# A mixture-of-experts block on one core: one-hot list products laid out tile by tile, with four experts' lists made ahead

## What is computed

```python
logits = flat_x @ gate_w.T
scores = softmax(logits, axis=-1).T               # (16, 8192)
topk_weight, topk_idx = top_k(scores, C)          # each expert picks its 1024 tokens
xg = flat_x[topk_idx]
h = gelu(xg @ Wg.T) * (xg @ Wu.T)                 # per expert, 1024 hidden
eo = (h @ Wd.T) * topk_weight[..., None]
out = scatter_add(zeros, topk_idx, eo)
shared = (gelu(x @ Sg.T) * (x @ Su.T)) @ Sd.T     # every token, 512 hidden
return x + layernorm(out + shared)
```

## Time and profile before

| | us |
|---|---|
| median of 3 runs | 2121.42 |
| lowest and highest | 2119.74, 2123.42 |
| profiled execution, whole time | 2122.61 |
| profiled execution, span from first to last instruction | 2120.8 |
| PE busy in the span | 2045.6 |
| DVE busy in the span | 1205.4 |

### The profile page before, as it was taken

The page is one execution under the profiler, slowest core; times in us unless marked ns, Lnnn a source line. Parts: engine busy times, 40 slices in busy tenths (PEclk is TensorE's granted clock), DMA queues, the critical chain, the costliest instruction groups (busy, mean ns, idle before and its releaser), DMA issues.

```text
span 2120.8 us, 33169 instructions
## 1 busy us (share of the span) xinstructions
PE 2045.6 (96%) x12826; PEld 1827.5 (86%) x12826; DVE 1205.4 (57%) x2527; ACT 968.2 (46%) x1802; POOL 439.4 (21%) x449
## 2 busy tenths in 40 slices
PE   7999999999995999999999999999999999999996
PEld 6899999999984887888898988888889898988885
DVE  5586686677663876454555555553443435353556
ACT  4464574565542333443434343434443434343544
POOL 0000000000001000222322331333233322322255
PEclk9999999999996999999999999999999999999999
DMA  3011111120115111332333333323333333334267
GB/s 112 1 41 42 61 62 48 52 80 41 41 41 201 60 61 40 105 80 66 68 76 74 77 74 76 79 72 70 84 79 76 76 78 79 76 91 100 51 191 136
DMA packets 55622, 159.94 MB, mean 75 GB/s; under 512 B 9536, under 2 KB 26048, under 8 KB 48320
## 3 DMA queue, kind: packets, MB, share of 16 engines
q1 hardware_dynamic: 28976, 116.16, 15.2%
q0 software_dynamic: 26512, 41.96, 12.4%
HBM read 98.78 MB, written 59.31 MB: 75 GB/s over the span
## 4 chain that ended last, share of the span: by engine, by line
PE 63%; DVE 2%; POOL 1%; ACT 1%; issue 1%; DMA 0%; DVEq 0%; SPq 0%; POOLq 0%; ACTq 0%
PE mo_psG L58 7%; PE mo_psD L58 7%; PE mo_psD L60 7%; PE mo_psD L59 7%; PE mo_psG L59 7%; PE mo_psG L60 7%; PE mo_psU L58 7%; PE mo_psU L60 7%; PE mo_psU L59 7%; PE mo_psX L967 1%; PE mo_psX L1151 1%; DVE mo_HF L1479 0%; DVE mo_st L1443 0%; DVE mo_XT_lo L1419 0%; POOL mo_rs L1735 0%
## 5 line engine op out<-in xcount | busy, mean ns | idle before, releaser
L1479 DVE TENSOR_TENSOR mo_HF<-mo_psU,mo_HF 128x512 f32<-128x512 f32 x320 | 221.2, 691 | 644.6 <-ACT mo_HF L1320 630.0
L1320 ACT ACTIVATE mo_HF<-mo_psG 128x512 f32<-128x512 f32 x320 | 191.5, 599 | 494.3 <-PE mo_psU L60 459.8
L1707 POOL DMA_INDIRECT ACC<-mo_OUT,mo_GI x128 | 205.8, 1608 | 666.3 <-ACT mo_OUT L1387 652.0
L60 PE MATMUL mo_psD<-mo_wd_hi,mo_H_lo 128*128 128x256 f32 x1024 | 289.8, 283 | 0.0
L59 PE MATMUL mo_psD<-mo_wd_lo,mo_H_hi 128*128 128x256 f32 x1024 | 289.8, 283 | 0.0
L58 PE MATMUL mo_psD<-mo_wd_hi,mo_H_hi 128*128 128x256 f32 x1024 | 289.6, 283 | 0.0
L1424 DVE TENSOR_TENSOR mo_H_lo<-mo_HF,mo_H_hi 128x512 fp32r<-128x512 f32 x300 | 204.5, 682 | 0.0
L1298 ACT ACTIVATE mo_H_hi<-mo_HF 128x512 fp32r<-128x512 f32 x320 | 199.4, 623 | 1.0 <-DVE mo_HF L1479 1.0
L59 PEld LDWEIGHTS mo_psD<-mo_wd_lo,mo_H_hi 128*128 128x128 f32 x1024 | 196.5, 192 | 1.2
L58 PEld LDWEIGHTS mo_psD<-mo_wd_hi,mo_H_hi 128*128 128x128 f32 x1024 | 196.5, 192 | 1.2
L60 PEld LDWEIGHTS mo_psD<-mo_wd_hi,mo_H_lo 128*128 128x128 f32 x1024 | 196.5, 192 | 0.0
(11 more groups left out here) (255 smaller groups left out, 5199.9 us busy)
## 6 DMA issues: line engine op xcount, KB each, us to landing
X1a<-wg_in SPq DMA_DIRECT2D x16, 1024.0 KB
X1a<-wu_in SPq DMA_DIRECT2D x16, 1024.0 KB, 4.9
X1a<-wd_in SPq DMA_DIRECT2D x16, 1024.0 KB
XN<-XNB SPq DMA_DIRECT2D x8, 1088.0 KB, 4.1
X<-x_in SPq DMA_DIRECT2D x8, 1024.0 KB, 6.4
out_dram<-X SPq DMA_DIRECT2D x8, 1024.0 KB, 4.4
XN2T<-xn2T SPq DMA_DIRECT2D x8, 1024.0 KB, 3.8
mo_F<-ACC SPq DMA_DIRECT2D x7, 1024.0 KB, 12.4
```

Of the source, the lines that this page charges most:

```text
L60: return pe.matmul(out, w_lo, x_hi, start=False, stop=last)
L1320: a.activation(HF[:, it % 2, :], psG[:, it % 2, :], ACT.Gelu).then_inc(s_gelu, 1)
L1479: v.tensor_tensor(HF[:, it % 2, :], psU[:, it % 2, :], HF[:, it % 2, :], ALU.mult).then_inc(s_mul, 1)
L1707: g.indirect_dma_start(out=io["ACC"], out_offset=bass.IndirectOffsetOnAxis(ap=GI[n % 2][:, 4 * tb + t:4 * tb + t + 1], axis=0), in_=OUT[:, ...
```

## The change

`VI` shrinks to one pair of columns for each slot. `hi1` and `val` take the layout that `lo1` has: 32 tiles x 32 slots x 2. All three DVE operations walk that layout. Their outputs are written through in order, and `VI` is read in runs of 64 that repeat for each tile. `LO`, `HI` and `TV` are read as a pair of neighbouring elements that repeats 32 times before the next pair comes. `p_list` takes `val` for one tile from 64 neighbouring elements.

`AHEAD` = 4 chunks are made beside the shared steps: their products run inside steps 34, 37, 38 and 41 (between G and U), and DVE's parts of them hang at 33.5, 34, 35, 37.5, 38, 39 and 41.5. Chunks 4 to 15 follow in expert blocks h = 0 to 11. On SP `store(0)` and `store(1)` come ahead of the stores of shared blocks 8 and 9, and `store(n + 1)` takes the place of `store(n)` among the loads of expert n.

```diff
+AHEAD = 2 * GCH
...
-        self.VI = new("VI", [P, SL, CW], BF16)
+        self.VI = new("VI", [P, SL, GE], BF16)
...
-        self.lo1 = new("lo1", [P, CW // GE, SL, GE], BF16)
-        self.hi1, self.val = new("hi1", [P, SL, CW], BF16), new("val", [P, SL, CW], BF16)
+        self.lo1, self.hi1, self.val = (new(n, [P, CW // GE, SL, GE], BF16) for n in ("lo1", "hi1", "val"))
...
         if x == 34:
+            self.v_acc(v, 0)
             self.v_lo1(v, 1)
         if x == 35:
-            self.v_acc(v, 0)
             self.v_hival(v, 1)
-        if x == 36:
+        if x == 37.5:
             self.v_acc(v, 1)
             self.v_dec(v, 0)
+            self.v_lo1(v, 2)
+            self.v_hival(v, 2)
+        if x == 38:
+            self.v_acc(v, 2)
+            self.v_lo1(v, 3)
+        if x == 39:
+            self.v_hival(v, 3)
+        if x == 41.5:
+            self.v_acc(v, 3)
+            self.v_dec(v, 1)
...
-        if x in (35, 36):
-            self.p_list(pe, x - 35)
+        if x in (33.75, 36.75, 37.75, 40.75):
+            self.p_list(pe, (33.75, 36.75, 37.75, 40.75).index(x))
...
-        split = lambda x: x.rearrange("p v (t e) -> p v t e", e=GE)
-        v.tensor_tensor(self.lo1[:, :, :, :].rearrange("p t v e -> p v t e"),
-                        split(self.LO[:, g, cols].unsqueeze(1).to_broadcast([P, SL, CW])), split(self.VI[:, :, :]),
-                        ALU.is_equal).then_inc(self.s_lo1, 1)
+        v.tensor_tensor(self.lo1[:, :, :, :], self.wide(self.LO[:, g, cols]), self.slots(), ALU.is_equal).then_inc(self.s_lo1, 1)
+
+    def wide(self, x):
+
+        return x.rearrange("p (t e) -> p t e", e=GE).unsqueeze(2).to_broadcast([P, CW // GE, SL, GE])
+
+    def slots(self):
+
+        return self.VI[:, :, :].unsqueeze(1).to_broadcast([P, CW // GE, SL, GE])
...
-        v.tensor_tensor(self.hi1[:, :, :], self.HI[:, g, cols].unsqueeze(1).to_broadcast([P, SL, CW]), self.VI[:, :, :],
-                        ALU.is_equal).then_inc(self.s_hi1, 1)
+        v.tensor_tensor(self.hi1[:, :, :, :], self.wide(self.HI[:, g, cols]), self.slots(), ALU.is_equal).then_inc(self.s_hi1, 1)
...
-        v.tensor_tensor(self.val[:, :, :], self.hi1[:, :, :], self.TV[:, cols].unsqueeze(1).to_broadcast([P, SL, CW]),
-                        ALU.mult).then_inc(self.s_val, 1)
+        v.tensor_tensor(self.val[:, :, :, :], self.hi1[:, :, :, :], self.wide(self.TV[:, cols]), ALU.mult).then_inc(self.s_val, 1)
...
-                          self.val[:, :, t * GE:(t + 1) * GE], start=(t == 0), stop=(t == tiles - 1))
+                          self.val[:, t, :, :].rearrange("p v e -> p (v e)"), start=(t == 0), stop=(t == tiles - 1))
...
-                    wait(pe, topk.s_acc, GCH)
+                    wait(pe, topk.s_acc, AHEAD)
...
-                    if it == 6 and 0 <= b - 1 - E0 < NCH - GCH:
-                        topk.p_list(pe, GCH + b - 1 - E0)
+                    if it == 6 and 0 <= b - 1 - E0 < NCH - AHEAD:
+                        topk.p_list(pe, AHEAD + b - 1 - E0)
...
-                if b == E0 - 2:
-                    topk.store(sp, 0)
+                if b in (8, 9):
+                    topk.store(sp, b - 8)
                 store(b)
...
-                if 1 <= n < GROUPS:
-                    topk.store(sp, n)
+                if 1 <= n < GROUPS - 1:
+                    topk.store(sp, n + 1)
```

More of the change, by code:

```diff
@@ L1506, in step @@
                             scores_of(expert(b)[0] + 1)
-                    if it == 7 and 0 <= b - 1 - E0 < NCH - GCH:
-                        topk.v_acc(v, GCH + b - 1 - E0)
+                    if it == 7 and 0 <= b - 1 - E0 < NCH - AHEAD:
+                        topk.v_acc(v, AHEAD + b - 1 - E0)
                 else:
@@ L1547, in down @@
                                 w_lo(w, 0, quarter)
[L1548 to L1552, removed]
+                if 0 <= h < NCH - AHEAD:
+                    topk.v_lo1(v, AHEAD + h)
+                    topk.v_hival(v, AHEAD + h)
+                if 0 < h <= NCH - AHEAD and h % GCH == 0:
+                    topk.v_dec(v, (AHEAD + h) // GCH - 1)
                 if b == D0:
```

## The result

| | median, us | lowest, highest | profiled execution, us | its span, us |
|---|---|---|---|---|
| before | 2120.58 | 2118.3, 2123.42 | 2122.61 | 2120.8 |
| after | 2097.5 | 2097.01, 2099.34 | 2097.01 | 2095.2 |

The ratio is 0.9892, with a 95% interval of 0.9875 to 0.9909: 23 us less (19.3 to 26.5 by the interval), where 10 were forecast.

The account below looks back on a forecast made before the run. PE was taken as the bound, busy 2045.6 of 2120.8 us. Terms 0 (PE layout), -4.2, +0.4 and -6.1 sum to -9.9, rounded to -10: 2121.42 to 2111.4, own range 2108 to 2115, 8-in-10 range 2099 to 2118.

Parts of the forecast that it names:

- Part 1: List products on PE: weights set the matmul spacing, so the new layout is worth 0; range 0 to -14 us.
- neither reading has the array's clock in it: List products take 1.98 us at clocks 1.00 and 0.50, so this cannot tell weight from moving columns as bound.
- The weights' reading: In list products the 64 weight columns set the matmul spacing of 0.056 us, 0.88 ns a column.
- The rival of the moving columns: On PE, scattered moving columns set list-product spacing: up to 14 us more gain, 2097 to 2106, say 2101; chance 0.2.
- halfway: In list products on PE, weights might stop the moving columns' gain short of its full 14 us.
- Part 2: DVE's one-hot operations take 1.23 us each, a chunk falls from 4.5 to 3.7; worth 0 in expert blocks.
- Part 3: Two products leave the expert blocks, -4.2 us; shared steps 34 to 41 take 43.5 against 43.1, +0.4.
- Part 4: Expert blocks: group 1's earlier list lets expert 2's gather begin near 963, ending PE's wait; -6.1 us.
- The second rival: DVE's repeated-pair reads take 2.08 us each; stage 14 to 18 longer, total +4 to +8; chance 0.1 including half case.

Follow-up runs that it names:

- order alone: New order (four chunks beside the shared MLP, stores one group ahead) with the layouts of before, against the kernel before: 2111.06 us against 2122.17, ratio 0.9953.
- layout alone: New layouts of hi1, val and VI with the order of before (two chunks beside the shared MLP), against the kernel before: 2105.7 us against 2122.17, ratio 0.9925.

## Why the prediction was wrong, point by point

- **Part 1, the layout on PE: wrong.** This is the step that failed, and it is the miss: I took the weights as what sets the distance of two matmuls, and so put the new layout at 0. The scattered moving columns set it (57 ns, and 32 when they are packed), and the term is -0.78 us for each of 16 products, or -0.83 by the distance of two expert blocks (36.45 to 35.62), 12.5 to 13.3 us in all. The forecast less that is 2098 to 2099, against 2097.5. I took the price of a weight column from gate products in fp32 and found it equal to that of the list products. The equality was an accident. The starts in the trace give 112 ns a record for the gate products with 128 weights, 0.88 a column (I had worked out 104, with 0.23 us for the last record, which lasts 0.26), and the added fp32 matmuls cost the same. But with bf16 64 contiguous weights fit in 32 ns. The list products' 57 were 32 pieces at 1.78 each. The rows of the two clocks, from which I took that "neither reading has the array's clock in it", were the better witness. The weights' reading does have it: the fp32 records, whose price is that of their weights (58 ns for 64, 112 for 128), go from 112 to 213 ns at 0.50 and the packed product from 32 to 53, while the product of before stayed at 57. That argument stood under the rival.
- The Trainium skill's rule for a weight load ("TensorE: Matmul & The Clock Gate", section "LDWEIGHTS (loading the stationary operand)"), columns by 1.2 GHz, was to decide between the readings. It gives 53 ns for 64 columns. The runs have 32 with 64 contiguous bf16 weights at a granted clock of 1.00, and 53 only at 0.50. The products of before ran at 1.00 but for one, so the measurement decides against the rule here.
- **The rival of the moving columns: right in its mechanism and its sum.** It gave 2097 to 2106 with 2101 as its value and a chance of 0.2, and 2097.5 lies at its lower end. Its floor of 0.028 us for a matmul was near the 0.032 measured, and "halfway" was not needed.
- **Part 2, the layout on DVE: right.** 1.22 us for each of the three, where 1.23 was forecast. The repeated pair costs nothing, which the row of the repeated element had said. The rule of the Trainium skill ("Vector Engine (DVE) Microarchitecture Reference", section 5.2) that a source hopping at every element is slower does not extend to a word that is read again: the operations take 1.22 us, not the estimated 1.9.
- **Part 3, four chunks: right within 0.3 us before Part 1's term.** With products of 2.1 the stage was to take 43.5. It takes 39.87, and four products at 0.83 less make 43.2. The waits for `val` were walked to 0, 0.4, 0.3 and 0.4; after shows none and three, 1.0 in all, no low clock. In order alone they were about 1.0 each, which the slower `lo1` explains.
- **Part 4, the late list: right.** Order alone gains 10.5 us in the expert blocks, of which 4.2 are two products and 6.3 the gather's wait with its clock, against 6.06 read off. POOL's copy was put near 963 and came at 955.54. The wait went and no next one appeared.
- **The second rival** had a price of 14 to 18 us if it came true. Made true by writes that lie apart, it cost 12.2 in the stage. The waits grew by 7.6 us (8.6 less 1.0) and not by 10; the clock, 4.6, lay within its 4 to 8. It left the kernel faster than before all the same, since the term that I had at 0 paid for it.

## What to carry to other kernels

Before calling an operand's layout free for TensorE, count the 16-byte pieces that one matmul's moving columns (and, apart from them, its weight columns) step through, and multiply by some 1.8 ns. If that is more than the matmul's other cost, it is the cost, and packing the columns side by side takes it away. Take the price of a short matmul only from rows of the same type; a spacing that is the same at both clock levels (57 ns here) points to the reads, and one that grows at 0.50 (32 to 53, 112 to 213) to the array.

## What the runs showed of the hardware that I had not expected

- A matmul with 64 contiguous weights and 64 moving bf16 columns costs 32 ns when the columns lie in 16 pieces of 16 bytes or fewer, 57 to 60 in 32 pieces, 110 to 116 in 64, at a granted clock of 1.00. Weights cost the same for the same pieces (60 in 32, 110 in 64), and the two don't add up (60 together).
- Two neighbours in a piece are not enough for full rate. The Trainium skill ("SBUF — State Buffer", section "Specifications (TRN2)") says that a line of 16 bytes needs two hits or more for full bandwidth. With bf16 columns two to a piece cost 57 to 60 ns and four to a piece 32, so on TensorE the runs disagree.
- Matmuls with 128 bf16 weights and 64 moving columns start 29 ns apart, those with 64 weights 32.
- A wait of PE of 2.21 us left the clock at 1.00 and one of 2.58 brought it to 0.50, in one and the same execution (layout alone). With slow one-hot operations, waits of 2.31 to 2.50 did so too.
- The clock also fell with no wait before it: PE was busy all through 931.30 to 934.50 with single moving columns 32 apart, and the product behind ran at 0.50. So it did behind single columns 8 apart and within both fp32 forms. Weights 32 apart, with the same 110 ns a matmul, left it at 1.00. A low granted clock by itself is therefore no sign that PE had waited.
